# Slot 2's product ahead of the marks, GpSimd's slot 1 ahead of the weights, and four smaller moves, in a convolution, scan and experts kernel

## The reference, cut to what matters

```python
x = x + conv(group_norm(x))
t = tokens(x)
# scan layer, on layer-normalised t
xc = silu(z @ W_conv + b_conv); gate = silu(x_gate)
dt = softplus(xc @ W_dt + b_dt)
h = exp(dt * A) * h + dt * B * xc        # 16 states for each of 128 channels, position by position
y = (h * C).sum(states) * gate
t = t + y @ W_out + b_out
# experts layer, on layer-normalised t
p = softmax(t_n @ Wr + br); two largest p, normalised, are the weights of two of 8 experts
t = t + sum over the two of weight * (gelu(xe @ W1 + b1) @ W2 + b2)
```

## Time and profile before

| | |
|---|---|
| median of 3 runs | 381.32 us (381.15 to 382.72) |
| the profiled execution | 379.5 us, its span 377.8 us |
| instructions in the span | 5525 |
| busy in the span: VectorE, TensorE, ScalarE, GpSimd | 316.5, 317.3, 277.9, 268.0 us |
| mean granted TensorE clock | 0.958 of full speed |
| one body of 2 to 5 | 36.9 us |

### The profile page before, as it was taken

One profiled execution on the slowest core, in us unless ns is written; L12 is line 12 of the kernel. 1 busy time (PEld: TensorE's weight loads), 2 busy tenths in 40 slices (PEclk: granted clock), 3 DMA queues, 4 the chain that ended last, 5 costly groups with the idle time before them and its releaser, 6 DMA issues. The chain is left out here.

```text
span 377.8 us, 5525 instructions
## 1 busy us (share of the span) xinstructions
PE 317.3 (84%) x1675; PEld 176.7 (47%) x1675; DVE 316.5 (84%) x424; ACT 277.9 (74%) x465; POOL 268.0 (71%) x268
## 2 busy tenths in 40 slices
PE   0597899695899889988998899989987997798795
PEld 0476455441555355525553455345534543453563
DVE  2784457998799989998999899989999998999533
ACT  1002458586989998989899989998988894872483
POOL 8903505685688978897799779977998787877110
PEclk9996999577899999999999999999998999999999
DMA  7934039979989989996996699769957985000000
GB/s 182 250 88 86 2 106 220 228 170 218 222 205 225 225 203 208 220 221 161 219 231 159 152 220 219 152 173 217 222 128 193 224 197 125 3 0 1 16 0 16
DMA packets 21301, 59.54 MB, mean 158 GB/s; under 512 B 4988, under 2 KB 13336, under 8 KB 15384
## 3 DMA queue, kind: packets, MB, share of 16 engines
q1 hardware_dynamic: 20104, 58.35, 68.1%
q10 hardware_dynamic: 1168, 0.84, 0.9%
HBM read 53.94 MB, written 5.24 MB: 157 GB/s over the span
## 5 line engine op out<-in xcount | busy, mean ns | idle before, releaser
L356 POOL TENSOR_TENSOR hs<-hs,Cs 128x1024 f32<-128x1024 f32 x63 | 149.3, 2376 | 22.5 <-DVE hs L836 21.8
L836 DVE TENSOR_TENSOR_SCAN hs<-av,P 128x1024 f32<-128x1024 f32 x64 | 146.3, 2286 | 2.6 <-POOL av L349 0.4
L830 DVE TENSOR_TENSOR P<-P,ub 128x1024 f32<-128x1024 f32 x62 | 76.0, 1226 | 3.1 <-DMA ub<-u_scratch 1.9
L676 ACT ACTIVATE hb<-P,b1c 128x512 f32<-128x512 f32 x112 | 70.1, 685 | 2.4 <-PE P L1309 1.0
L1321 PE MATMUL P<-hb,W2s 128*64 128x256 f32 x448 | 60.3, 392 | 0.0
L1308 PE MATMUL P<-X,W1H 128*128 128x512 f32 x112 | 49.6, 443 | 4.3 <-ACT hb L676 3.3
L617 ACT ACTIVATE av<-P,Aneg 128x510 f32<-128x510 f32 x68 | 44.1, 680 | 9.3 <-PE P L1241 5.2
L1309 PE MATMUL P<-X,W1L 128*128 128x512 f32 x112 | 44.5, 398 | 0.0
L1321 PEld LDWEIGHTS P<-hb,W2s 128*64 128x64 f32 x448 | 27.4, 136 | 27.8 <-issue 17.3
L617 ACT ACTIVATE av<-av,Aneg 128x510 f32<-128x510 f32 x60 | 38.3, 708 | 2.6 <-DMA av<-dt_scratch 2.5
L1241 PE MATMUL P<-D,selD 128*128 128x512 f32 x64 | 29.9, 509 | 11.7 <-ACT av L617 11.4
(11 more groups left out here) (230 smaller groups left out, 546.3 us busy)
## 6 DMA issues: line engine op xcount, KB each, us to landing
ub<-u_scratch SPq DMA_DIRECT2D x31, 1024.0 KB, 11.5
av<-dt_scratch SPq DMA_DIRECT2D x15, 1024.0 KB, 7.3
dt_scratch<-dts SPq DMA_DIRECT2D x7, 256.0 KB, 2.9
u_scratch<-rl SPq DMA_DIRECT2D x7, 256.0 KB, 2.9
av<-in_L_conv_Wr SPq DMA_DIRECT2D x2, 576.0 KB, 6.9
av<-in_L_conv_Wl SPq DMA_DIRECT2D x2, 576.0 KB, 8.6
res<-in_x SPq DMA_DIRECT2D x4, 256.0 KB, 4.5
hb<-in_L_ffn_W SPq DMA_DIRECT2D x2, 512.0 KB, 5.9
```

The lines of the kernel that those rows point to most:

```text
L356: gp.tensor_tensor(hs[:, at, :, :], hs[:, at, :, :], rep(Cs[:, p, :], 1, 2), ALU.mult).then_inc(S["cm"], 1)
L676: a_.activation(hb[:, r % HB, :], P[:, F1_BANK[r], :], ACT.Gelu, bias=b1c[:, r:r + 1]).then_inc(S["gl"], 1)
L830: v.tensor_tensor(ring, rep(P[:, BB, :], 1, 2), ub[:, 2 * n:2 * n + 2, :], ALU.mult).then_inc(S["bm"], 1)
L836: v.tensor_tensor_scan(hs[:, (SLOTS * g + n) % RING].rearrange("p a t -> p (a t)"), av[:, 2 * n:2 * n + 2, :].rearrange("p a t -> p (a t)" ...
```

## The change

- VectorE: the slot is split into its product and its scan. Slot 2's product goes ahead of the marks, slot 7's ahead of the third weighting.
- GpSimd: slot 1's multiply goes between the split and the weights, with a wait for the split.
- ScalarE: decays 0 to 3 of `nxt` all come ahead of softplus.
- TensorE: `pe_proj` takes the two images one after the other, and the first waits for all gelus but the last; row 10 of f2 moves behind it.
- The tail's input: VectorE makes xn first, GpSimd copies the high part of one image from it, VectorE makes that of the other, then both low parts. The output's second half is issued by ScalarE's queue.

```diff
--- before.py
+++ after.py
@@ -273,9 +273,9 @@
                     sp_.wait_ge(S["u_out"], 16 * (g + 1))
                 sp_.dma_start(ub[:, 4 * c:4 * c + 4, :], rep(u_dram[p][:, 4 * c:4 * c + 4, :], 0, ST)).then_inc(S[f"u_in{c}"], 16)
 
-        def sp_out(sp_, g, p):
+        def sp_out(sp_, g, p, halves=(0, 1)):
             sp_.wait_ge(S["acc"], EXP * (g + 1))
-            for h in range(2):
+            for h in halves:
                 sp_.dma_start(ov[h, :, g:g + 1, :], acc[64 * h:64 * h + 64, 0:1, :]).then_inc(S["out_sem"], 16)
 
         @block.sync
@@ -328,7 +328,7 @@
                 sp_spread(sp_, g, g % 2)
                 sp_out(sp_, g - 2, g % 2)
             sp_out(sp_, G - 2, 0)
-            sp_out(sp_, G - 1, 1)
+            sp_out(sp_, G - 1, 1, (0,))
             sp_.wait_ge(S["out_sem"], 32 * G)
 
 
@@ -512,9 +512,11 @@
                     step_input(eng, gp, nxt, q)
                 if prev is not None:
                     pool_x2(eng, prev)
-                    pool_router(eng, prev)
+                    eng.wait_ge(S["xl2"], prev + 1)
                 if i > 0:
                     pool_slot(eng, i, p, 1)
+                if prev is not None:
+                    pool_router(eng, prev)
                 pool_slot(eng, i, p, 2)
                 pool_slot(eng, i, p, 3)
                 pool_slot(eng, i, p, 4)
@@ -541,6 +543,9 @@
 
             for i in range(G):
                 body(i, i % 2, i + 1 if i + 1 < G else None, i + 2 if i + 2 < G else None, i - 1 if i > 0 else None)
+            eng.wait_ge(S["xn2"], 2 * G)
+            eng.wait_ge(S["f1"], LAST)
+            gp.tensor_copy(X2[0:64, 0:HW], xn[0:64, :]).then_inc(S["xh2"], 1)
             pool_router(eng, G - 1)
 
 
@@ -758,12 +763,10 @@
                     act_silug(eng, nxt2)
                 a_.preload_act_table_set("natural_log_exp_and_others")
                 if nxt is not None:
-                    act_decay(eng, nxt, 0, 1)
+                    act_decay(eng, nxt, 0, 1, 2, 3)
                 if nxt2 is not None:
                     act_abs(eng, nxt2)
                     act_softplus(eng, nxt2)
-                if nxt is not None:
-                    act_decay(eng, nxt, 2, 3)
 
             act_lnA1(eng, 0, XA)
             act_lnA2(eng, 0, XA)
@@ -809,12 +812,18 @@
                 act_wbt(eng, 2 * n + 1)
                 for r in range(4 * n + 8, 4 * n + 12):
                     act_gelut(eng, r)
+            sp_out(eng, G - 1, 1, (1,))
 
 
         ring = P[:, 0:2, :]
         MIXED = (XA, XB, 0, 1)
 
         def dve_slot(eng, g, n):
+
+            dve_product(eng, g, n)
+            dve_scan(eng, g, n)
+
+        def dve_product(eng, g, n):
 
             c = n // 2
             if n == 0:
@@ -828,6 +837,10 @@
                     eng.wait_ge(S[f"u_in{c}"], loads(c, g))
                 since(eng, "scan", SLOTS * g + n)
                 v.tensor_tensor(ring, rep(P[:, BB, :], 1, 2), ub[:, 2 * n:2 * n + 2, :], ALU.mult).then_inc(S["bm"], 1)
+
+        def dve_scan(eng, g, n):
+
+            c = n // 2
             eng.wait_ge(S["bm"], SLOTS * g + n + 1)
             eng.wait_ge(S["aexp"], NBLK * g + 2 * n + 2)
             if n % 2 == 0:
@@ -1085,8 +1098,10 @@
                 if prev is not None:
                     dve_xn1(eng, prev)
                     dve_router1(eng, prev)
+                dve_product(eng, i, 2)
+                if prev is not None:
                     dve_router2(eng, prev, nxt2)
-                dve_slot(eng, i, 2)
+                dve_scan(eng, i, 2)
                 if i == 0:
                     dve_relu(eng, 1)
                 if i == 0:
@@ -1101,8 +1116,9 @@
                     dve_xn(eng, 2)
                 experts(2)
                 dve_slot(eng, i, 6)
+                dve_product(eng, i, 7)
                 experts(4)
-                dve_slot(eng, i, 7)
+                dve_scan(eng, i, 7)
                 if nxt is None:
                     last = hs[:, (SLOTS * G - 1) % RING, :, :]
                     eng.wait_ge(S["cm"], SLOTS * G - 1)
@@ -1118,14 +1134,12 @@
             eng.wait_ge(S["rq"], G)
             eng.wait_ge(S["xl2"], G - 1)
             eng.wait_ge(S["f1"], LAST)
-            for h in range(2):
-                q = slice(64 * h, 64 * h + 64)
-                v.tensor_tensor(X2[q, HW * h:HW * h + HW], P[q, XB, 0:HW], rqs[q, :], ALU.mult).then_inc(S["xh2"], 1)
             v.tensor_tensor(xn, P[:, XB, 0:HW], rqs[:, :], ALU.mult).then_inc(S["xn2"], 2)
+            v.tensor_tensor(X2[64:128, HW:T], P[64:128, XB, 0:HW], rqs[64:128, :], ALU.mult).then_inc(S["xh2"], 1)
             eng.wait_ge(S["xn2"], 2 * G)
-            eng.wait_ge(S["xh2"], 2 * G)
-            for h in range(2):
+            for h in (1, 0):
                 q, o = slice(64 * h, 64 * h + 64), slice(64 - 64 * h, 128 - 64 * h)
+                eng.wait_ge(S["xh2"], 2 * G)
                 low = v.tensor_tensor(X2[o, HW * h:HW * h + HW], xn[q, :], X2[q, HW * h:HW * h + HW], ALU.subtract)
             low.then_inc(S["xl2"], 1)
             dve_router2(eng, G - 1)
@@ -1171,15 +1185,14 @@
             eng.wait_ge(S["xn1"], g + 1)
             eng.wait_ge(S["sp_relu"], g)
             eng.wait_ge(S["aexp"], NBLK * (g - 1))
-            since(eng, "gl", EXP * KC * (g - 2))
             eng.wait_ge(S["b1c"], 1)
             eng.wait_ge(S["wrc"], 1)
             for h in range(2):
-                last = pe.matmul(P[:, (XA, XB)[h], 0:HW], Wzs[64 * h:64 * h + 64, h, :], xnt[64 * h:64 * h + 64, :], start=True, stop=True)
-            last.then_inc(S["z_mm"], 1)
-            for h in range(2):
-                last = pe.matmul(P[:, (XA, XB)[h], HW:T], Wgs[64 * h:64 * h + 64, h, :], xnt[64 * h:64 * h + 64, :], start=True, stop=True)
-            last.then_inc(S["g_mm"], 1)
+                since(eng, "gl", EXP * KC * (g - 2) - 1 + h)
+                z = pe.matmul(P[:, (XA, XB)[h], 0:HW], Wzs[64 * h:64 * h + 64, h, :], xnt[64 * h:64 * h + 64, :], start=True, stop=True)
+                gate = pe.matmul(P[:, (XA, XB)[h], HW:T], Wgs[64 * h:64 * h + 64, h, :], xnt[64 * h:64 * h + 64, :], start=True, stop=True)
+            z.then_inc(S["z_mm"], 1)
+            gate.then_inc(S["g_mm"], 1)
 
         def pe_projg(eng, g):
             if g == 1:
@@ -1524,7 +1537,7 @@
                     pe_f2(eng, prev, 0)
                     pe_f2(eng, prev, 1)
                     pe_wt(eng, prev)
-                    for n, (fill, back) in enumerate(((4, (2, 3)), (6, (4, 5)), (8, (6,)), (10, (7, 8)), (12, (9,)), (14, (10,)))):
+                    for n, (fill, back) in enumerate(((4, (2, 3)), (6, (4, 5)), (8, (6,)), (10, (7, 8)), (12, (9,)), (14, ()))):
                         pe_f1(eng, prev, fill)
                         pe_f1(eng, prev, fill + 1)
                         for r in back:
@@ -1536,7 +1549,7 @@
                 if nxt2 is not None:
                     pe_proj(eng, nxt2)
                 if prev is not None:
-                    for r in range(11, 16):
+                    for r in range(10, 16):
                         pe_f2(eng, prev, r)
                 if i == 0:
                     for k in range(3):
```

## The result

The changed kernel takes 390.37 us (median of four executions, 387.88 to 390.69) against 382.02 us of the kernel before (four, 381.15 to 385.41): a ratio of 1.020, 95% interval [1.016, 1.024]. Six more executions, run later, gave 388.36 us (386.26 to 390.76), ratio 1.017 [1.011, 1.022]. So the change makes the kernel slower, as forecast, but by 5.6 to 8.4 us where the forecast had 3.0.

A forecast was written before the change was run, and what follows sets the result against it. Bound: a loop of waits, GpSimd's chain from scan 5 to the gate, VectorE's from gate to scan 5. 2.0 + 0.9 + 1.0 - 0.4 - 0.5 = +3.0 us; on the 381.3 median, 384.3 us, range 380.9 to 386.2.

The forecast's parts named there:

- L902 waits for the whole rest of slot 1: VectorE's small tensor_scalar at the marks, 0.16 us before, ends only with GpSimd's slot 1 multiply, at about 215.9 in body 4.
- +0.43 per body: Scan 2 on VectorE starts at 216.37 against 215.93, lengthening each body; counted as +2.0 us for bodies 1 to 5.
- Body 6: Scan 2 comes 1.21 us later, less VectorE's 0.29 wait for ScalarE's weights: +0.9 us.
- Body 7: Scan 2 comes 1.1 us later, less 0.1 from product 7 ahead of the third weighting: +1.0 us.
- Body 1 and what lies ahead of it: Body 1 has a shorter distance, but was counted at 0.4 us longer; no term was given for the stretch ahead.
- The tail: After the last gate: -0.4 us from sharing the input's operations, -0.5 us from issuing half the output on ScalarE's queue.
- Decays and projections at 0 on the loop: ScalarE's earlier decays: 0; TensorE's split projections and later row 10: -0.3 to +0.3 us on TensorE, 0 on the loop.
- A: Rival at VectorE's L902: no wait, or a fixed 0.16 us; bodies of 35.8, 374.0 us in all; chance 0.17.
- B: Rival: L902 waits, but VectorE's path sets the gate, not GpSimd's; no change, 382.5 us; chance 0.15.
- C: Rival: weights come too late for TensorE's transposes; five bodies each lose another 0.5 us, 386.8 us; chance 0.04.

The follow-up runs named there:

- e5: Changed kernel with GpSimd's old order (slot 1 behind the weights) and row 10 of f2 ahead of the projections again; 377.31 us, ratio to before 0.987.
- e3: Changed kernel in its whole new order, but L915 writes its four elements to PSUM and the reciprocal reads them there; 377.87 us, ratio to before 0.987.

## Why the prediction was right in direction and wrong in size

**L902 waits for the whole rest of slot 1: right.** I took that from one instance of L902 and from L960. It was so in seven bodies, and the old order, the new order alone and the PSUM version (0.16 beside the running multiply) show that it is the cause. The Trainium skill, page "SBUF — State Buffer", section "Who interferes with whom", has it as a rule: where a tensor_scalar takes the ports that VectorE shares with GpSimd, whichever of the two comes second is blocked for the whole instruction of the other. The trace agrees: L915 took 1.90 us and ended 0.03 after the multiply.

**+0.43 per body: right.** Measured 0.48, with 0.57 instead of 0.50 from GpSimd's end to the scan. Body 6: +0.85 where I said +0.9. Body 7 without the fall at its gate: 35.44 - 34.28 = +1.16 where I said +1.0.

**Body 1 and what lies ahead of it: not settled.** I counted +0.4 for body 1 and nothing ahead of it. The profile has +0.99 and +3.25, but these stretches differ nearly as much between executions without this change: the time to body 1's gate was 92.8 to 95.7 in the other thirteen profiles (94.53 in the changed kernel's second), and body 1 took 37.4 to 40.2 in those without the wait at L915. What of this is the change's can't be read from single executions.

**The tail: right but a little high.** -0.72 instead of -0.9. The input gave what I said (1.90 instead of 2.28 from the start of the input's first operation to f1); the output's two parallel issues gave 0.38, not 0.5: from the first issue to the end are 2.60, against 2.98 before.

**Decays and projections at 0 on the loop: nearly right.** Alone they cost 0.1 per body. With the products moved they come to 36.33 against 36.30 without them, as "about cancel" had it: row 10 of f2 behind the projections costs 0.37 (forecast 0.47), and the rest gives 0.34. Row 10 could have stayed where it was: with that, e5 has bodies of 35.96.

**The step that failed is the sum itself: it has no term for TensorE's clock, and gives no reason for leaving it out.** I costed each term on an execution with a clock of 0.958, the highest of the kernel before, and added 1.8 for the median of the runs shown; so the changed kernel was given the clocks of the kernel before. It did not have them. Over 49 executions of the kernel before, 0.01 less mean clock goes with 1.8 us more (a line through them; correlation -0.79; mean clock 0.949). The changed kernel's ten have a mean of 0.934, so by an estimate from that line 1.5 x 1.8 = 2.7 us of its loss go with the clock. The lower clock goes with L915's wait and not with the other moves: e3, which differs only in where L915 writes, has a mean of 0.950 in its four executions. In the first profile two falls can be priced by rows: body 7, 37.84 - 35.44 = 2.40, and the last stretch 1.36. That the second goes with a longer wait for VectorE is seen at that gate; why body 7 lost its clock in one profile and not in the other is open.

The rest: 1.91 + 0.85 + 1.16 - 0.72 and some 0.5 for body 1 make 3.7, against the forecast's 3.0. With 2.7 for the clock that is 6.4; the two comparisons measured 8.4 and 5.6, so up to 2.0 of the first stays unexplained. The base was low too: the forecast started from 381.3, the median of three executions, and the medians of the kernel before in the five comparisons are 382.0 to 382.8.

**The rivals.** A (no wait, 374.0, bodies of 35.8) was wrong for this kernel, and came near for one that writes L915 to PSUM: 36.3 and 377.9 us, or 35.95 and 375.8 with row 10 put back and the four matmuls added. What limits those bodies first is TensorE's slot sums, not ScalarE's row as A had it. B needed bodies of 37.0 with no wait at the gate; there is one of 0.23, and 37.4. C: the weights were not late: no weighting of VectorE waits (L931 in the lines), and ScalarE's first copy of a row waits 0.64 where it waited 0.65.

## What to carry to other kernels

Before moving a long GpSimd instruction earlier, list VectorE's operations that will then run beside it: here a tensor_scalar with both ends in SBUF waited for all of it, small as it is, and a PSUM output for its four elements took the wait away. When TensorE's clock moves between executions, regress time on clock over all the runs there are, and give the forecast a term for it; one profile shows where the clock fell, not that the change made it fall. A cure that works in one profile is run again, beside the uncured kernel.

## What the runs showed of the hardware that was not expected

The output's place alone decided whether the tensor_scalar waited: its input stayed in SBUF. TensorE's granted clock fell to half behind idle times of 1.37, 1.78, 1.85, 2.19 and 2.27 us in some executions, and stayed full behind 1.82 to 1.85 and 2.24 in others at the same places, so a single idle time does not tell whether it falls. Behind such a fall the same four matmuls took 0.95 to 1.12 us instead of 0.65.
